# Gate products in column strips, direct gate transfers, causal zeros on the scores and a written-out loop in the second attention of a fused two-layer block

## The reference

```python
# second sublayer: h is the gated hidden layer, 6 tiles of 128 rows (the last one short)
h = clip(round(h / scale), -128, 127)        # scale from the largest |h|
x = x + h @ w_down * scales
# third sublayer: q = layernorm(x), k = v = ctx, for each batch and head (dh = 64)
gate_in = concatenate((q, ctx, ctx))         # 768 features
ig, fg = gate_in @ ik + ib, gate_in @ fk + fb            # one number per token and head
cs = cumsum(log_sigmoid(fg))
log_d = where(tri, cs_i - cs_j + ig_j, neg)
m = max_j(log_d); d = exp(log_d - m)
c = q @ k.T / 8 * d
n = maximum(sum_j(c), exp(-m))
h = c / (n + eps) @ v                        # then RMS norm and scale, added to x
```

## Time and profile before

| | us |
|---|---|
| runs: 791.32, 793.56, 793.77; median | 793.56 |
| the profiled execution | 792.24 |
| span of the profiled execution | 790.5 |
| first attention, feed-forward, up to the scale of the hidden layer | 0 to 236.6 |
| rounding, down products, third layer norm | 236.6 to 269.7 |
| gates, up to the 64 rows being on chip | 269.7 to 296.3 |
| decay chain, broadcast, start of the loop | 296.3 to 325.8 |
| loop over the batches | 325.8 to 383.4 |
| routing | 383.4 to 420.0 |
| experts | 420.0 to 790.5 |

### The profile page before, as it was taken

One profiled execution on the slowest core, in us unless ns is written; L12 is line 12 of the kernel. 1 busy time (PEld: TensorE's weight loads), 2 busy tenths in 40 slices (PEclk: granted clock), 3 DMA queues, 4 the chain that ended last, 5 costly groups with the idle time before them and its releaser, 6 DMA issues.

```text
span 790.5 us, 16899 instructions
## 1 busy us (share of the span) xinstructions
PE 656.0 (83%) x4582; PEld 456.3 (58%) x4582; DVE 505.7 (64%) x1269; ACT 383.9 (49%) x894; POOL 277.6 (35%) x297
## 2 busy tenths in 40 slices
PE   3899999995765775577317999999999999999991
PEld 2788888873323335477313666666666666666661
DVE  6588999997687456688693464646464555564441
ACT  1466666655869335476224443645353545443320
POOL 3111111220354402544202363637364545563311
PEclk9899999998898997555557999999999999999997
DMA  9100000003000006111371514262434353512214
GB/s 283 37 14 13 13 14 14 7 0 106 2 0 0 1 9 230 30 34 27 127 247 29 187 28 139 77 182 47 135 81 133 83 147 81 188 28 35 35 15 119
DMA packets 45682, 58.89 MB, mean 74 GB/s; under 512 B 13296, under 2 KB 39216, under 8 KB 45328
## 3 DMA queue, kind: packets, MB, share of 16 engines
q1 hardware_dynamic: 38128, 47.79, 18.5%
q0 software_dynamic: 7488, 10.31, 7.5%
HBM read 145.90 MB, written 11.80 MB: 199 GB/s over the span
## 4 chain that ended last, share of the span: by engine, by line
PE 56%; DVE 18%; issue 10%; ACT 5%; DMA 4%; POOL 3%; DVEq 2%; ACTq 1%; SPq 0%; POOLq 0%
PE psum L1000 19%; PE psum L1022 10%; PE psum L708 4%; PE psum L1013 3%; PE psum L692 3%; PE psum L715 3%; PE psum L728 2%; ACT region L1271 2%; PE psum L697 1%; PE psum L747 1%; DMA region<-neg_max_dram 1%; PE psum L735 1%; DVE region L1893 1%; POOL region L590 1%; PE psum L891 1%
## 5 line engine op out<-in xcount | busy, mean ns | idle before, releaser
L1000 PE MATMUL psum<-region 128*128 x936 | 217.1, 382 | 1.0 <-DVE region L1889 1.0
L1000 PEld LDWEIGHTS psum<-region 128*128 128x128 bf16 x936 | 92.2, 98 | 96.5 <-issue 4.1
L1254 ACT ACTIVATE region<-psum 128x512 f32<-128x512 f32 x78 | 46.5, 596 | 182.0 <-PE psum L1000 182.0
L636 POOL DMA_INDIRECT sum_dram<-region,row_token x39 | 74.5, 1911 | 133.7 <-DVE region L1885 133.7
L1022 PE MATMUL psum<-region 128*128 x936 | 109.1, 273 | 5.6 <-DVE region L1893 5.6
L1022 PEld LDWEIGHTS psum<-region 128*128 128x128 bf16 x936 | 90.4, 98 | 18.8 <-issue 8.2
L1868 DVE TENSOR_TENSOR region<-psum,region 128x512 f32<-128x512 f32 x78 | 53.9, 691 | 69.9 <-ACT region L1254 69.8
L529 POOL TENSOR_TENSOR region<-region,pair_mask 128x256 f32<-128x256 f32 x32 | 21.3, 687 | 127.5 <-ACT region L1061 127.5
L628 POOL DMA_INDIRECT region<-xrow_dram,row_token x39 | 40.9, 1048 | 55.1 <-DVE row_token L1863 27.2
L1893 DVE TENSOR_TENSOR region<-psum,region 128x1024 bf16<-128x1024 f32 x39 | 47.6, 1222 | 17.7 <-ACT region L1262 17.7
L1347 DVE TENSOR_REDUCE region<-psum 128x8 f32<-128x1024 f32 x32 | 39.0, 1220 | 17.7 <-PE psum L708 17.7
(11 more groups left out here) (291 smaller groups left out, 1208.3 us busy)
## 6 DMA issues: line engine op xcount, KB each, us to landing
region<-in_L_ffn_w SPq DMA_DIRECT2D x117, 1024.0 KB
region<-in_ctx SPq DMA_DIRECT2D x32, 128.0 KB, 2.5
region<-neg_max_dram SPq DMA_DIRECT2D x2, 1536.0 KB, 9.8
xrow_dram<-region SPq DMA_DIRECT2D x1, 2080.0 KB, 8.3
x_sb<-in_x SPq DMA_DIRECT2D x4, 512.0 KB, 6.8
region<-in_ctx SPq DMA_DIRECT2D x2, 1024.0 KB, 6.9
sum_dram<-x_sb SPq DMA_DIRECT2D x1, 2048.0 KB, 7.5
region<-neg_max_dram SPq DMA_DIRECT2D x1, 768.0 KB, 5.8
```

Source lines behind the costliest of these rows:

```text
L636: pool.indirect_dma_start(sum_dram, bass.IndirectOffsetOnAxis(ap=row_token[:, t:t + 1], axis=0), y_d[:, t % 2, :], None, compute_op=ALU.ad ...
L1000: last = mm(psum[:, 2 * f + n, :], (xT_lo if xl else xT_hi)[:, p, k, :], weights_at(place, wl, n, k * F1 + f * FH, FH), start=(i == 0), st ...
L1254: act_fn(sil_d[:, f, :], psum[:, 2 * f, :], ACT.Silu).then_inc(sil_d_ready, 1)
```

## The change

- The hidden layer is cut in nine pieces: two of 128 tokens, then seven of 256. VectorE rounds pieces 0, 1, 2, 4, 6 and 8 alone with two operations each; ScalarE starts 3, 5 and 7 and VectorE clips them. ScalarE still writes all of them as bf16. The statistics of pairs 1 to 7 stand behind the last read of down products; the power -1/2 is taken in three lots (8, 4, 4 batches), all behind the residual adds. The statistics go straight to their place, without the copy.
- The gate kernels are padded with zeros from 8 to 32 columns (column 8h + n), and the four groups write four strips of 32 partitions in one bank (6). The ctx products run slice by slice over the four groups, the x products run once behind all x transposes. One copy (128x512) and two transfers straight from gates_all to gates8 take the place of four copies, eight stores and one load. The rows are then in the order group, head, batch. The scores no longer wait for the gate copies.
- `causal` writes zeros on ST after each read of scores, and `decay_scores` takes min(decay, 1) times ST. The decays wait for the broadcast alone. The broadcast parts are by batch 0; 1 to 3; 4 to 7; 8 to 11; 12 to 15, the first four batches as four transfers with 4 separate rows each. SPLIT_1 is 4.
- The loop is written out on all engines. The statistics' copy is gone there too, and the router's norm is written straight to xrow: the transposes read it there and ScalarE's second copy is gone.

```diff
-    SPLIT_1, SPLIT_2 = 5, 8
-    GATE_BANK = (2, 3, 6, 7)
+    SPLIT_1, SPLIT_2 = 4, 8
+    GATE_BANK = 6
-    MAX_PARTS = ((0, 1), (1, 4), (4, 10), (10, 16))
+    MAX_PARTS = ((0, 1), (1, 4), (4, 8), (8, 12), (12, 16))
+    H_PIECES = (slice(0, P), slice(P, 2 * P)) + tuple(slice(n * TB // 2, (n + 1) * TB // 2) for n in range(1, 2 * G))
+    H_ON_ACT = (3, 5, 7)
+    X2_LOTS = (slice(0, B // 2), slice(B // 2, EARLY), slice(EARLY, B))
...
# SP
-            for g in range(G):
-                sp.wait_ge(gates_read, g + 1)
-                for n in range(2):
-                    sp.dma_start(gates_dram[n, g * GB:(g + 1) * GB, :, :].rearrange("b h n -> h b n"),
-                                 gates_all[n * H1:(n + 1) * H1, g * TB:(g + 1) * TB].rearrange("h (b n) -> h b n", n=P)).then_inc(gates_stored, 16)
-            sp.wait_ge(gates_stored, 32 * G)
-            sp.dma_start(gates8[0:B * H1, 0:2, :], gates_dram.rearrange("g b h n -> (b h) g n")).then_inc(gates_loaded, 16)
+            sp.wait_ge(gates_read, 1)
+            for n in (1, 0):
+                sp.dma_start(gates8[0:B * H1, n, :], gates_all[n:n + 8 * (G * H1 - 1) + 1:8, :]).then_inc(gates_loaded, 16)
...
+            for n, (first, end) in enumerate(MAX_PARTS):
+                sp.wait_ge(st_done, max(end, GB))
+                for rows in [slice(b, GB * H1, GB) for b in range(first, end)] if first < GB else [slice(first * H1, end * H1)]:
+                    source = neg_max_dram[rows, :]
+                    sp.dma_start(neg_max[:, rows, :], source.unsqueeze(0).to_broadcast([P] + list(source.shape))).then_inc(neg_max_loaded[n], 16)
...
# POOL
             def causal(b):
-                part = neg_max[:, bass.ds(H1 * b, H1), :]
-                nc.gpsimd.affine_select(out=part, in_=part, compare_op=ALU.is_ge, fill=NEG, base=0,
+                pool.wait_ge(st_read, b + 1)
+                part = ST[:, H1 * b:H1 * (b + 1), :]
+                nc.gpsimd.affine_select(out=part, in_=part, compare_op=ALU.is_ge, fill=0.0, base=0,
                                         pattern=[[0, H1], [1, P]], channel_multiplier=-1).then_inc(masked_ready, 1)
-            for g, (first, end) in enumerate(MAX_PARTS):
-                pool.wait_ge(neg_max_loaded[g], 16)
-                for b in range(first, end):
-                    causal(b)
+            for b in range(B):
+                causal(b)
...
# PE
+            def gate_columns(g):
+                return psum[32 * g:32 * (g + 1), GATE_BANK, :]
+            def gates_ctx():
                 for k in range(KT):
+                    for g in range(G):
+                        mm(gate_columns(g), gk_ctx[:, k, :, :].rearrange("p h n -> p (h n)"), cT_all[:, g * GB:(g + 1) * GB, KT + k, :], start=(k == 0), stop=False)
...
             for j in range(B // 2):
                 x_transposes_c(j)
-                if j >= 2 and j % 2 == 0:
-                    gates_x(j // 2 - 1)
-            gates_x(G - 1)
-            pe.wait_ge(gates_read, G)
+            gates_x()
...
# ACT
             act.wait_ge(gu_ready, 2)
+            hidden_store(0)
+            hidden_store(1)
+            hidden_round(3)
+            hidden_store(2)
+            hidden_round(5)
+            hidden_store(3)
+            hidden_store(4)
+            hidden_round(7)
+            hidden_store(5)
+            hidden_store(6)
+            hidden_store(7)
+            hidden_store(8)
...
# DVE
+            def hidden_round(i):
+                part = hT[:, :, H_PIECES[i]]
+                link(nc.vector.tensor_scalar(part, part, act_inv[:, 1:2], QMAX, ALU.mult, ALU.min))
+                nc.vector.tensor_scalar(part, part, -QMAX - 1.0, MAGIC, ALU.max, ALU.add).then_inc(h_clipped, 1)
...
+            hidden_round(0)
+            hidden_round(1)
+            hidden_round(2)
+            hidden_clip(3)
             down_scaled(0, 0, first=True)
+            hidden_round(4)
             down_scaled(1, 1, first=True)
+            hidden_clip(5)
+            hidden_round(6)
+            down_scaled(2, 0)
+            hidden_clip(7)
+            down_scaled(3, 1)
+            hidden_round(8)
+            down_scaled(4, 0)
+            down_scaled(5, 1)
+            down_scaled(6, 0)
             pair_stats(0)
+            down_scaled(7, 1)
...
             def decay_scores(b, p, inner=False):
+                dve.wait_ge(masked_ready, b + 1)
                 dve.wait_ge(decay_ready, b + 1)
...
-                nc.vector.tensor_tensor(decayed[:, p, :, :], ST[:, bass.ds(H1 * b, H1), :], decay[:, p, :, :],
-                                        ALU.mult).then_inc(decayed_ready, 1)
+                nc.vector.scalar_tensor_tensor(out=decayed[:, p, :, :], in0=decay[:, p, :, :], scalar=1.0, in1=ST[:, H1 * b:H1 * (b + 1), :],
+                                               op0=ALU.min, op1=ALU.mult).then_inc(decayed_ready, 1)
```

More of the change, by code:

```diff
@@ L309, in build @@
         neg_max_ready = sem("neg_max_ready")
-        neg_max_loaded = [sem(f"neg_max_loaded{i}") for i in range(4)]
+        neg_max_loaded = [sem(f"neg_max_loaded{i}") for i in range(5)]
         floor_ready = sem("floor_ready")
@@ L962, in _ @@
             values_c(1, 1, 1, 1)
-            for b in range(PEEL):
-                step_c(b, b % 2, b % 4, loads=b // 2 + 2)
-            with pe.Fori(PEEL // 4, TAIL // 4) as i:
-                for q in range(4):
-                    step_c(4 * i + q, q % 2, q, loads=2 * i + (q // 2 + 2), inner=True)
-            for b in range(TAIL, B + 3):
+            for b in range(B + 3):
                 step_c(b, b % 2, b % 4, loads=b // 2 + 2)
@@ L1198, in decays @@
                     n = H1 * b + h
-                    last = act_fn(decay[:, p, h, :], neg_max[:, bass.ds(n, 1), :].rearrange("p o c -> p (o c)"), ACT.Exp,
+                    row = GB * H1 * (b // GB) + GB * h + b % GB
+                    last = act_fn(decay[:, p, h, :], neg_max[:, row, :], ACT.Exp,
                                   bias=aT[:, bass.ds(n, 1)])
@@ L1462, in gate_kernels @@
                 dve.wait_ge(gk_loaded, 16 * (4 + 2 * B))
-                nc.vector.tensor_tensor(gk_ctx[:], gk[:, KT:2 * KT, :], gk[:, 2 * KT:3 * KT, :], ALU.add).then_inc(gk_ready, 1)
+                dve.wait_ge(gk_ready, 2)
+                for n in range(2):
+                    part = slice(n * H1, (n + 1) * H1)
+                    nc.vector.tensor_copy(gk_x[:, :, :, n], gk[:, 0:KT, part]).then_inc(gk_ready, 1)
+                    nc.vector.tensor_tensor(gk_ctx[:, :, :, n], gk[:, KT:2 * KT, part], gk[:, 2 * KT:3 * KT, part], ALU.add).then_inc(gk_ready, 1)
                 nc.vector.tensor_scalar_add(rms1[:], rms1[:], 1.0)
@@ new lines, in _ @@
+            hidden_round(6)
[6 more added lines that the diff above has]
+            down_scaled(6, 0)
+            pair_stats(0)
+            down_scaled(7, 1)
+            for n in range(1, B // 4):
+                pair_stats(n)
+            x2_eps(0)
+            for n in range(B // 4, EARLY // 2):
+                pair_stats(n)
+            x2_eps(1)
+            for n in range(EARLY // 2, B // 2):
+                pair_stats(n)
```

167 lines of the change are left out of this document (62 added, 105 removed).

## The result

The changed kernel takes 772.86 us (median of 4 runs, 770.96 to 775.29), the kernel before in the same job 793.66 (791.32 to 794.45): a ratio of 0.9744, 95% interval 0.9707 to 0.9782. The forecast was 771.4, with a range of 764 to 779. The profiled execution of the changed kernel took 774.13 (span 772.3), 18.1 less than the profiled one of before (792.24, span 790.5).

A forecast was written before the change was run, and what follows sets the result against it. Around the second attention no engine is full, so order and waits set the time. Nine terms (0, -5.6, -6.3, -1.7, +1.6, +0.7, -4.6, -5.6 with -0.3, +1) sum to -20.8, taking 792.24 to 771.4 us; range 764 to 779.

The forecast's parts named there:

- Rounding and statistics: Rounding pieces and statistics up to the first norm: four adds collide with VectorE's roundings, 3.8 us; 0 us gained.
- Rival A: Rounding stage: no collisions, so the norm starts 3.8 us earlier and the total is 767.6; chance 0.13.
- Order of the ctx products: Gates: ctx products in strips end before the norm comes, so x transposes start at 270.5; -5.6 us.
- rival C: Gates: the strips don't run side by side, x products take 7 in place of 2; 779.5 us; chance 0.06.
- x stage and clock: x transposes to gates copy: 15.5 becomes 9.2, -6.3 us; TensorE's clock may fall for part of it, +1.
- Rival B: TensorE's clock stays low from the x transposes to the scores: 5.5 us, total 776; chance 0.13.
- Transfers: Gates copy to gates on 64 rows: two on-chip transfers land in 1.5 to 4 us; -1.7 us.
- Decay chain: Decay chain: one score read moves in, +0.75, and collisions with GpSimd's `causal`, +0.85; +1.6 us.
- step 9: TensorE's clock: idle ahead of the x transposes may lower it for part of the x stage; +1 us (0 to 5).
- Causal off the start: Loop start: second residual add no longer waits for `causal`, -4.6 us; v of batch 2 is late next.
- The loop: Loop written out: 14 steps fall from 3.95 to 3.55 us each; -5.6 us.
- Rivals D and E: Loop: D, bound elsewhere, steps near 3.95, 777 us, chance 0.06; E, slower from fetching written-out code, chance 0.02.

The follow-up runs named there:

- small-adds run: Changed kernel with GpSimd adding only the first of the 256 features to x for the first four pairs of batches: 771.99 us, ratio 0.9693.
- two-queue run: Changed kernel with the second gate transfer (the input gates) issued from ScalarE's queue instead of behind the first on SyncE's: 771.89 us, ratio 0.9735.

## Why the prediction was right, step by step

The number was 1.5 us under the median, 0.2%. Its sum, -20.8, stands against -18.2 between the profiled executions, of which the stages that the change touches have -20.4, and against -20.8 between the medians of one job; the agreement of the last is partly luck, since the two profiled executions lie 1.3 on opposite sides of their medians.

1. **Rounding and statistics**, 0 forecast, -0.3 measured. Four operations are stretched (1.91, 2.03, 1.44 and 1.90), in three roundings and not in four, by 3.3 us together where I had 3.8, and the small-adds run shows the cause. Rival A, no collisions, is out: the adds do meet the roundings. Had they not, TensorE's products would have taken back 0.8 of it, which A left out.
2. **Order of the ctx products**, -5.6 and -5.4: the x transposes now wait for one pair of norms, 1.01, and no longer for the ctx products. The strips took 1.92, at the low end of what I gave them; rival C is out. (The Trainium skill's factor for three tiles, in TensorE: Matmul & The Clock Gate, "Measured speedup vs the span model", would have made it 3.0. It does not carry over to four strips: here it was 3.66.) No run undoes the strips or the moved gate products, so steps 2 and 3 rest on the marks in the two timelines.
3. **x stage and clock**, -6.3 + 1 against -5.5 together. The clock fell, for a part of the stage, at the price of 0.9. Where it doesn't fall, the stage is 9.13 against a worked-out 9.2. Rival B gave a low clock 5.5. In these profiles it cost 1.6: 0.9 in the x stage and 0.7 in the decay chain, by scores at half clock. One of my signs of being wrong did come there: two score reads 0.85 apart with the clock at half (289.03 and 289.88).
4. **Transfers**, -1.7 against -0.6. This step failed: I took "1.5 to 4 us" to land and then let VectorE's four reads, 3.0, be later than it. The gates landed 4.0 after the copy and VectorE stood 1.29. The upper end of a range that I had named myself was the value, and the landing more than 3 us after the copy was a sign that I had named. What held the last packets back was an instruction packet, which no term had. The two-queue run, at 2.65, is what the step described.
5. **Decay chain**, +1.6 and +1.6, but the agreement is luck. Where the clock is full up to the third score the stage takes 5.8, so the two causes that I named are worth 0.9 and not 1.6: one more score read, 0.6, and one scan that collides, 0.33 (0.75 for 0.42), where I had 0.75 and 0.85. The other 0.7 is the wait for scores at half clock, which I had put into step 9.
6. **Broadcast**, +0.7 against +1.0, but this stage was 16.9 to 20.1 in the versions with two value buffers, so neither number is told from the other.
7. **Causal off the start**, -4.6 against -4.9 in the stages; undone, +3.7. "v of batch 2 is late next" was right, and it cost 3.2 more.
8. **The loop**, 3.55 a step forecast, 3.53 measured, and +6.2 when undone. Rivals D and E (slow steps, or waits for instructions) are out: no step of the changed kernel is over 3.6 in either profile. (One step of the two-queue run took 3.80; I don't know why.)

## What to carry to other kernels

Price a removed operation by what then releases the one that waited for it: context products that fell from 7.03 to 1.92 us, and now end ahead of the norm, gave 5.4 here, all of the wait behind the norm but for one pair of norms. The saved score read and the shorter transfers gave a third of what was forecast, because the transfer itself was late next. After each edit ask which wait is next on the chain. Here these were three that the profile of the changed kernel named outright (statistics behind a rounding that ScalarE had time for, a value operand queued behind a broadcast, a late second transfer on one queue), and their removal was worth another 8 us in the medians of one job. Before a stage's agreement with its forecast counts as proof, look at the granted clock in it: two causes of 0.9 and a low clock of 0.7 made up my +1.6. Where GpSimd and VectorE share a stage, look at the maximum beside the median of a line: a factor of two was a collision here each time. A wait on GpSimd's side, where it has slack, ended the one that it was placed for.

## What the runs showed that I had not expected

- Column strips don't need alternating products: with both products of a strip in a row, 16 instructions took 1.95 us, alternating 1.92, in one strip 7.03.
- Two small transfers issued from one queue landed 4.0 us after the copy, and from two queues by 2.65, a gain of twice the issue time of 0.64. The traces show why: the last four of their packets came behind a 16 KB instruction packet of 0.9 to 1.4 us. So what else was on the DMA engines set this landing time, 3.0 to 3.6 us from the issue with that packet and 1.9 without.
- The granted clock of the same instructions differs between executions: the x stage was at full clock in some, and at 0.72 for 6 of its 10 us in the changed kernel's first profile, 0.9 us apart. Some of the executions with the full clock there had lost as much in the down products before.
- The collision goes both ways: GpSimd's 128x512 add takes 1.27 us alone, and up to 1.98 beside VectorE's roundings.
